# Output projection of a state-space layer: four full float32 products per tile become twelve reduced-precision ones

## What is computed

```
proj = rmsnorm(layernorm(x)) @ in_proj_w.T        # z 512, x_ssm 512, B 128, C 128, dt 8 columns
xc   = silu(conv4(x_ssm) + conv_b)                # per channel, four taps over time
dt   = softplus(dt_raw + dt_bias);  dA = exp(-exp(A_log) * dt)
h_t  = h_{t-1} * dA_t + (dt_t * xc_t) B_t ;  y_t = h_t C_t     # 8 heads of 64, state 128
y    = (y + D * xc) * silu(z)
out  = layernorm(x) + y @ out_proj_w.T            # 512 -> 256 channels; x = x + out
```

## Time and profile before

| | |
|---|---|
| runs | 1993.59, 1994.06, 1997.53 us; median 1994.06 |
| the profiled execution | 1994.79 us, its span (first to last instruction) 1992.6 us |
| PE, DVE, ACT, POOL busy in the span | 87%, 68%, 57%, 46% |
| state-space layer, first silu of xc to the end | 1411.5 to 1766.5 us |
| starts of the silu of xc (L1641) | 1411.49, 1458.08, 1504.23, 1550.39, 1596.53, 1642.69, 1688.91, 1733.92 us |
| granted clock of PE, mean | 0.961 of full speed |

### The profile page before, as it was taken

How to read it: one execution, slowest core, us unless ns; L and a number is a source line. 1 busy time by engine, 2 the same in 40 slices (tenths; PEclk the granted TensorE clock), 3 DMA queues, 4 the chain that set the end, 5 groups by cost and what they waited for, 6 DMA issues and landing times. The chain is left out here.

```text
span 1992.6 us, 30608 instructions
## 1 busy us (share of the span) xinstructions
PE 1740.4 (87%) x9553; PEld 1146.7 (58%) x9600; DVE 1364.6 (68%) x2907; ACT 1133.7 (57%) x1624; POOL 912.7 (46%) x621
## 2 busy tenths in 40 slices
PE   4999674899898998988899889997888888879998
PEld 3888564223222222225788767775666666657776
DVE  3544663677777777775545578885788887778886
ACT  3322463999999999995323222222777777622221
POOL 0001341899999999993000342211455444431111
PEclk9999887899999999999899989998999999989999
DMA  4000136424435352410000100000333222200000
GB/s 147 0 0 11 48 111 147 75 43 72 56 55 72 42 81 45 63 22 0 11 0 0 43 17 1 0 0 13 115 99 96 85 85 85 91 28 22 21 11 32
DMA packets 57638, 96.91 MB, mean 49 GB/s; under 512 B 7937, under 2 KB 29665, under 8 KB 57569
## 3 DMA queue, kind: packets, MB, share of 16 engines
q1 hardware_dynamic: 54752, 93.45, 20.8%
q10 hardware_dynamic: 2816, 2.60, 0.6%
HBM read 78.98 MB, written 17.04 MB: 48 GB/s over the span
## 5 line engine op out<-in xcount | busy, mean ns | idle before, releaser
L1217 POOL TENSOR_TENSOR att_weights<-att_weights 128x1024 f32<-128x1024 f32 x288 | 541.2, 1893 | 34.6 <-DVE att_weights L1161 23.6
L1161 DVE SCALAR_TENSOR_TENSOR att_weights<-att_weights,ps 128x512 f32<-128x512 f32 x576 | 370.2, 684 | 169.3 <-ACT att_weights L1136 167.5
L1132 ACT ACTIVATE att_weights<-ps 128x1024 f32<-128x1024 f32 x288 | 294.4, 1022 | 26.7 <-PE ps L1078 22.9
L1136 ACT ACTIVATE att_weights<-att_weights 128x1024 f32<-128x1024 f32 x288 | 302.5, 1051 | 0.0
L711 DVE SCALAR_TENSOR_TENSOR X<-ps,moe_gsel,X 128x256 f32 (+1 forms) x512 | 246.8, 484 | 66.5 <-PE ps L47 50.7
L1092 PE MATMUL ps<-att_weights,att_v_ones 128*32 128x512 f32 (+3 forms) x1536 | 288.7, 497 | 2.6 <-POOL att_weights L1217 2.5
L1075 PE MATMUL ps<-att_q_stack,att_k_stack 128*128 128x512 bf16 (+3 forms) x721 | 215.7, 334 | 51.6 <-DVE att_weights L1161 43.0
L1075 PEld LDWEIGHTS ps<-att_q_stack,att_k_stack 128*128 128x128 bf16 x768 | 74.3, 97 | 321.6 <-DVE att_weights L1161 285.0
L47 PE MATMUL ps<-w_experts_hi,moe_xh 128*128 128x512 f32 x512 | 206.2, 403 | 0.3 <-DVE X L711 0.3
L47 PE MATMUL ps<-w_experts_hi,moe_xl 128*128 128x512 f32 x512 | 203.9, 398 | 0.0
L47 PE MATMUL ps<-w_experts_lo,moe_xh 128*128 128x512 f32 x512 | 202.3, 395 | 0.0
(11 more groups left out here) (252 smaller groups left out, 3749.0 us busy)
## 6 DMA issues: line engine op xcount, KB each, us to landing
att_q_stack<-qk_parts SPq DMA_DIRECT2D x128, 128.0 KB, 4.6
ssm_lb<-decays SPq DMA_DIRECT2D x32, 512.0 KB, 4.8
ssm_rise<-decays SPq DMA_DIRECT2D x32, 512.0 KB, 3.9
att_k_stack<-qk_parts SPq DMA_DIRECT2D x120, 128.0 KB, 7.7
qk_parts<-qkv_part SPq DMA_DIRECT2D x32, 384.0 KB, 2.6
out<-X SPq DMA_DIRECT2D x8, 512.0 KB, 2.9
X<-in_x SPq DMA_DIRECT2D x3, 1024.0 KB, 5.7
load_raw<-in_ffn_w SPq DMA_DIRECT2D x8, 256.0 KB, 5.2
```

Of the source, the lines that this page charges most:

```text
L1132: act.activation(Wt[:, u % WU], scores(u), ACT.Exp).then_inc(exp_done, 1)
L1136: act.activation(Wt[:, u % WU], Wt[:, u % WU], ACT.Ln, bias=1.0).then_inc(ln_done, 1)
L1161: dve.scalar_tensor_tensor(out=wt[:, t], in0=wt[:, t], scalar=LIMIT, in1=scores(u)[:, t], op0=ALU.min, op1=ALU.max).then_inc(max_done, 1)
L1217: pool.tensor_tensor(Wt[:, u % WU], Wt[:, u % WU], Wt[:, u % WU], ALU.mult).then_inc(sq_pool, 1)
```

## The change

The weights of the output projection are kept as two F32R parts, `out_h` and `out_l`. They are loaded into the first slot of `dec`, and at the start of the layer ACT copies the high part and DVE subtracts for the low part. `y` becomes one slot. After `gate`, ACT copies `y` into `yh` (`high`), then DVE subtracts into `yl` (`remainder`) and signals `y_done`; `gate` itself signals `yg_done`. `tile_out` takes twelve products with 256 columns from the four parts. The wait for `out_done` moves from `gate` on DVE to `high` on ACT, and asks for the tile just before.

```diff
-        out_w, ones = sb("out_w", [P, FT, C]), sb("ones", [P, P])
+        ones = sb("ones", [P, P])
+        out_h, out_l = (sb(f"out_w_{part}", [P, FT, C], F32R) for part in ("hi", "lo"))
...
+        out_w = dec[:, 0].rearrange("p h t -> p (h t)").rearrange("p (f c) -> p f c", f=FT)
...
-        y = sb("y", [P, 2, FT, P])
+        y = sb("y", [P, FT, P])
+        yh, yl = (sb(f"y_{part}", [P, FT, P], F32R) for part in ("hi", "lo"))
...
-                for k in range(FT):
-                    ins = pe.matmul(ps_o, y[:, b % 2, k], out_w[:, k], start=k == 0, stop=k == FT - 1)
-                ins.then_inc(out_done, 1)
+                matmul3(pe, ps_o, lambda k: yh[:, k], lambda k: yl[:, k], lambda k: out_h[:, k],
+                        lambda k: out_l[:, k], range(FT)).then_inc(out_done, 1)
...
+            pe.wait_ge(out_split, 1)
             groups(pe, group)
...
+            def high(n, b):
+
+                act.wait_ge(yg_done, n + 1)
+                act.wait_ge(out_done, 2 + n)
+                act.activation(yh[:, :, :], y[:, :, :], ACT.Copy).then_inc(yh_done, 1)
+
...
                     if left and b == 0:
                         hi(p + 1)
+                    high(n, b)
                     if left and b:
                         piece(p + 1, 1 - v, b)
...
             act.activation(neg_a[:, :], neg_a[:, :], ACT.Exp).then_inc(init_done, 1)
+            act.activation(out_h[:, :, :], out_w[:, :, :], ACT.Copy).then_inc(oh_done, 1)
             hi(0)
...
+            act.wait_ge(out_split, 1)
             decays(0, 0, 0, 0)
...
                 dve.wait_ge(y_summed, n + 1)
-                dve.wait_ge(out_done, n + 1)
...
-                dve.tensor_tensor(y[:, b % 2], y[:, b % 2], zs[:, :, b], ALU.mult).then_inc(y_done, 1)
+                dve.tensor_tensor(y[:, :, :], y[:, :, :], zs[:, :, b], ALU.mult).then_inc(yg_done, 1)
+
+            def remainder(p, b):
+                n = p * GT + b
+                dve.wait_ge(yh_done, n + 1)
+                dve.tensor_tensor(yl[:, :, :], y[:, :, :], f32(yh[:, :, :]), ALU.subtract).then_inc(y_done, 1)
...
                     gate(p, v, b)
                     update_state(p, v, b)
+                    remainder(p, b)
...
+            dve.wait_ge(oh_done, 1)
+            dve.tensor_tensor(out_l[:, :, :], out_w[:, :, :], f32(out_h[:, :, :]), ALU.subtract).then_inc(out_split, 1)
             dve.wait_ge(init_done, 4)
             statistics(1)
```

More of the change, by code:

```diff
@@ L1403, in ssm_phase @@
                              "state_done", "h_decayed", "h_done", "out_done", "x_done"))
+        yg_done, yh_done, oh_done, out_split = (sem(n) for n in ("yg_done", "yh_done", "oh_done", "out_split"))
         FREE = 1
@@ L1755, in gate @@
                 dve.wait_ge(y_summed, n + 1)
-                dve.wait_ge(out_done, n + 1)
                 for f in range(FT):
-                    ins = dve.scalar_tensor_tensor(out=y[:, b % 2, f], in0=xc[:, v, f, b], scalar=d_col[:, f:f + 1],
+                    ins = dve.scalar_tensor_tensor(out=y[:, f], in0=xc[:, v, f, b], scalar=d_col[:, f:f + 1],
                                                    in1=ps_y[:, f * P:(f + 1) * P], op0=ALU.mult, op1=ALU.add)
```

## The result

| | runs of this comparison, us | median |
|---|---|---|
| before | 1993.59 to 2001.49 (4 runs) | 1995.8 |
| after | 2026.89 to 2030.37 (4 runs) | 2028.34 |

The changed kernel is slower: ratio 1.0159, 95% interval 1.0135 to 1.0184, 32.5 us between the medians. Its profiled execution took 2028.83 us with a span of 2027.0, 34.4 more than the earlier trace rows.

A forecast was written before the change was run, and what follows sets the result against it. It put PE on the path only in part, with gate hand-overs, ACT's order and DVE deciding elsewhere. 24.6 + 1.6 + 3.9 + 2.0 = 32.1 us on 1994.79 gave 2026.9, 2026 for the median; range 2019 to 2033.

The forecast's parts named there:

- six steady groups: Groups with a normalise: waits at tiles 0 to 3 and the end make each 4.1 us longer, 24.6 in all.
- the seventh group: Group without normalise: the copy of tile 3 waits only for its gate, +1.6 us.
- The last group: Nothing hides its hand-overs: four of 1.5 us, less 0.4, less about 1.7: +3.9, between 1.5 and 5.6.
- The product term: Output projection on PE: twelve split products at 0.12 us take 1.43 for 1.83, a gain of 0.40 us per tile.
- Tile 0: Steady group: tile_y(1) starts 1.5 us later behind copy and subtraction; decays(2), behind the copy on ACT, 3.7 later.
- Tile 1: Steady group: PE's units, tile_y(2), decays(3) and weigh(3) all at +1.1 us; DVE's idle 4.83 us hide the rest.
- Tile 2: Steady group: ACT reads the two x_ssm units only after gate and copy, +3.9 us; decays(4) and normalise slip too.
- The end of a group: Steady group: ACT is 4.7 us late at the silu of xc, but DVE at times_dt(0) sets the shift, +4.1.
- The fourth rival: The subtraction meets POOL on the path: 2.2 us more in each of six groups, 2039; 8%.
- less about 1.7: Last group: PE's waits of 1.60 us come from a 2.7 us multiply beside POOL, which the later gate partly escapes.
- The third rival: New waits around tile_out(3) lower PE's clock at each group's start: +10 us over six groups, 2036; 15%.
- The start of the layer: ACT's weight copy and DVE's subtraction stand ahead of statistics and first operands: +2.0 us, between 1.2 and 2.6.

The follow-up runs named there:

- e1: The kernel before with twelve F32R products, DVE's multiply writing y as F32R, no copy or subtraction, high part used for both: 1995.58 us, ratio 0.9995.
- e2: The changed kernel with copy, subtraction and their waits, but the four float32 products of before: 2029.62 us, ratio 1.0159.
- e5: The changed kernel with tile_y waiting for the gate's four additions, not for the end of the subtraction: 2018.35 us, ratio 1.0108.
- e7: As e5, with the projection of the tile before placed behind tile_state and turn_x on PE: 2017.07 us, ratio 1.0103.
- e9: As e2, with ACT's copy alone and no subtraction; the copy signals y_done: 2022.55 us, ratio 1.0137.
- e11: The changed kernel with POOL's long product cut to an eighth, the rest left out of the result: 2014.02 us, ratio to before 1.0085.
- e3: The changed kernel with ACT's copy of tile 2 moved behind the two units of x_ssm: 2026.02 us, ratio 1.0147.
- e10: As e2, with DVE's subtraction alone, reading y alone, and no copy on ACT: 2017.99 us, ratio 1.0109.
- e12: The kernel before with POOL's long product cut to an eighth, the rest left out of the result: 1984.96 us, ratio 0.9948.
- light pair: e11 and e12, the changed kernel and the one before with POOL's long product cut to an eighth: 2014.02 and 1984.96 us.
- e6: The kernel before with tile_y waiting for the gate's four additions, not for the multiply behind them: 1997.76 us, ratio 1.0008.

## Why the prediction was right

The time, 2026 for 2028.3, came out, and so did the mechanism of the six steady groups but for the engine that comes last in them. Part of the nearness is luck: in the profiled execution the six groups and the start were 3.5 us under their terms, the seventh group, the last and what stands ahead of the layer 5.9 over. The last group, 7.3 us, lies outside its own bounds of 1.5 to 5.6.

**The product term.** PE's gain per tile was 0.30 us and not 0.40: the 0.12 us between starts were right, but the first product costs 0.22. It changed little: by e1 the whole gain is worth 0.17 us a group.

**The chain, shown by its length.** In six kernels ACT has no gap from the copy of tile 2 to the silu, and this stretch is always 17.6 us. The group's length is then the end of the gate of tile 2 (all times after the group's silu) plus that stretch: after 32.16, e2 32.51, e5 31.12, e7 31.15, e9 31.83, e11 31.00, and the groups 49.79, 50.13, 48.75, 48.77, 49.45, 48.63. Each sum agrees within 0.03 us. Before, the gate ended at 31.57, nearly the same, but the stretch did not wait for it. That is the prediction's tile 2, "the wait that costs".

**Tile 0.** Measured from the group's silu, `decays(2)` started at 10.53 for 7.46. After starts each group 0.55 us sooner in one respect: `tile_y(0)` follows the silu at 4.82, not 5.37, since DVE no longer is last there. So +3.6, forecast +3.7. The wait of PE before `tile_y(1)` ended with the subtraction, as forecast.

**Tile 1.** exp of dt started at 22.03 for 21.46, +1.1 with the same 0.55 counted, as forecast; DVE's idle 4.83 us shrank to 1.64.

**Tile 2.** `normalise` at 39.03 for 35.92: +3.65, forecast +3.9.

**The end of a group: the wrong engine.** The prediction had ACT 4.7 late at the silu and DVE setting the shift at 4.1. ACT was 3.62 late and sets it; DVE, with `cb` at 49.19 for 46.11, was 3.08 late. With the 0.55 us counted, ACT was 4.2 and DVE 3.6 late, each half a microsecond under its forecast, and it is luck that DVE's forecast 4.1 is near ACT's 4.2. The 0.55 us that a group gets back at its start make 3.6 of that: 2.9 us less than forecast over six groups.

**The seventh group.** Forecast +1.6, since the copy of tile 3 has no `normalise` to wait for. It didn't, but the gate and a convolution met POOL:

```profile
1750.09 2.36 POOL L1863 TENSOR_TENSOR ssm_rise<-ssm_rise,ssm_cT 128x1024 f32<-128x1024 f32 x1
1750.20 2.79 DVE L1775 TENSOR_TENSOR ssm_y<-ssm_y,ssm_zs 128x512 f32<-128x512 f32 x1
...
1753.73 2.91 POOL L1863 TENSOR_TENSOR ssm_rise<-ssm_rise,ssm_cT 128x1024 f32<-128x1024 f32 x1 [1.28 <-DMA ssm_rise<-decays]
...
1754.63 4.14 DVE L1725 SCALAR_TENSOR_TENSOR ssm_xc<-ssm_xpad,ssm_conv_w,ssm_xc 128x512 f32<-128x512 f32 x3
```

These are 2.1 and 1.8 us over 0.69 and 2.32, with DVE last at the silu. They are not all new: before, the same multiply took 1.82, and the convolution and the small copy behind it at tile 2 took 2.98 and 2.32 for 2.32 and 0.17. Without these two the changed kernel has room for its hand-overs, and the gate's additions of tile 3 start 36.5 us after the silu in both kernels. From there the multiply is 1.0 longer, the subtraction with its wait adds 0.8, and the convolution is 1.8 longer: 3.6. The fourth rival looked for the collision at the subtraction, which after never shows (753 ns at the longest; in e3 and e10 it does). It fell on other instructions of DVE, in a group without its cover. In e11, without most of POOL's product, this group took 44.35 us for 48.58, in e12 42.38 for 45.01: by these runs the collisions are 1.6 of the 3.6, and 2.0 stay.

**The last group.** Forecast +3.9 (1.5 to 5.6), measured +7.3. The term was "four of 1.5", less 0.4, "less about 1.7". DVE after, at tiles 1 to 3:

```profile
1774.44 1.65 DVE L1756 TENSOR_TENSOR ssm_dec<-ssm_dec,ssm_cb 128x1024 f32<-128x1024 f32 x1 [2.07 <-ACT ssm_dec L1614]
...
1782.96 1.23 DVE L1756 TENSOR_TENSOR ssm_dec<-ssm_dec,ssm_cb 128x1024 f32<-128x1024 f32 x1 [1.74 <-ACT ssm_dec L1614]
1784.16 1.12 DVE L1770 SCALAR_TENSOR_TENSOR ssm_y<-ssm_xc,ssm_d_col,ps 128x128 f32<-128x128 f32 x4
...
1793.28 1.13 DVE L1770 SCALAR_TENSOR_TENSOR ssm_y<-ssm_xc,ssm_d_col,ps 128x128 f32<-128x128 f32 x4 [3.39 <-PE ps L1494]
```

- The hand-over of 1.5 is right at tile 0 and too short behind it. `decays(2)` and `decays(3)` stand behind the copies of tiles 0 and 1, and DVE's `weigh` and with it the gate wait for them, 2.07 and 1.74 us, where before the one wait of this kind was 0.60. The prediction had named this order for the steady groups and left it out here. In the light pair, where no `tile_y` up to these starts runs slow, `tile_y` to `tile_y` is 5.46, 7.75 and 7.75 us in e11 for 4.01, 5.12 and 4.79 in e12: +1.5, +2.6, +3.0.
- The "less about 1.7" came to 0.9: the multiply of tile 1 took 1.69 us for 2.69, that of tile 2 took 2.80 for 2.68.
- The clock was not in the term. PE after, at tiles 2 and 3, and `tile_y(3)` in e3, whose last group has the same order on every engine:

```profile
1780.44 0.70 PE L1491 MATMUL ps<-ssm_dec,ssm_xdt 128*64 128x128 f32 x4 [3.63 <-DVE ssm_y_lo L1780]
1780.89 0.67 PE L1494 MATMUL ps<-ssm_rise,ssm_H 128*64 128x128 f32 x4
...
1789.71 0.69 PE L1491 MATMUL ps<-ssm_dec,ssm_xdt 128*64 128x128 f32 x4 [2.19 <-DVE ssm_y_lo L1780]
```

```profile
1786.00 0.44 PE L1491 MATMUL ps<-ssm_dec,ssm_xdt 128*64 128x128 f32 x4 [2.30 <-DVE ssm_y_lo L1783]
```

The clock over that place and over a `tile_y` at full speed, from the windows view of the changed kernel (columns as above):

```profile
1781.00:1783.00 2.00, 2.00 (x22) 2.00 (x20) 0.26 (x2) 1.90 (x4) 0.00 (x0) 0.50 0.04 8
1773.00:1774.00 1.00, 1.00 (x18) 0.83 (x14) 0.00 (x0) 0.97 (x3) 0.04 (x1) 1.00 0.06 25
```

At tiles 2 and 3 the groups of four products start 0.42 us apart where 0.22 is usual, the granted clock is 0.50, 1.2 GHz, and a `tile_y` takes 3.26 us from its first start to its last for 1.70. `tile_y(0)` runs slow as well, but it did so before too; the mean clock of the window is 0.82, before 0.95. At tile 2 the slow clock costs nothing that the rows show: the additions at 1784.16 follow `weigh` without a gap. At tile 3 DVE waits for PE, and there e3 gives the price: its `tile_y(3)` ran at full clock, and from that start to the end of the layer it took 8.43 us where the changed kernel took 10.00. So of the 3.4 us missed the clock is 1.6, the multiply that did not escape POOL 0.8, and about 1 the `decays` behind the copies. e3 was not made to test this, and no experiment held the clock up.

The third rival had the mechanism and the wrong price. Behind PE's wait of 2.6 us `tile_y(3)` ran slow in four of the six groups too. Over the five from the second silu the mean clock was 0.97 in three and 1.00 in two, and they took 49.75 to 49.84 and 49.76 to 49.77 us: ACT's stretch ends later than PE there, and the +10 us did not come. In the seventh group, also at 0.50, DVE waited 0.84 us for this `tile_y`. Not each gap brought the low clock: in the last group of e9 `tile_y(2)` ran at full clock behind 3.86 us. The Trainium skill (TensorE: Matmul & The Clock Gate, Why this matters for your kernels) warns of idle gaps between bursts; the last group agrees with it, and e9 shows a gap that cost no clock.

**The start of the layer** was +1.4 to the first silu: copy 1.04 at 1381.14 and subtraction 1.23 at 1382.21 on ACT and DVE, statistics at 1383.35 for 1381.06, +2.3. Of these 0.5 stood ahead of the layer and 0.4 were covered.

## What to carry to other kernels

A saving on the busiest engine is worth nothing until some place shows that engine as the one that comes last: here 0.30 us of PE per tile bought 0.17 us a group, and a copy of 0.63 us with a subtraction of 0.69 cost 3.6 us a group. When a wait is put into an engine's written order, ask what stands behind it and where that stretch ends; an unbroken stretch like ACT's 17.6 us moves whole with its first instruction. Where two chains end within a microsecond of each other, relieving one shows only the small gap to the other, and parts tried alone (3.3 and 2.2 us) do not add up to the whole (4.0).

## What the runs showed of the hardware

- Twelve F32R products of 256 columns with weights that change at every product started 0.12 us apart, as in the earlier trace rows, but 0.22 behind the first; the four float32 ones took 0.46 each. Up to the next instruction the change of form is worth 0.30 of 1.83 us.
- DVE beside POOL: a 128x512 multiply of 0.69 us took 2.8, a convolution of three steps 6.85 for 2.32, a copy of 128x512 to F32R 2.28 for 0.42. The Trainium skill (SBUF — State Buffer, SBUF: two separate sides) has a VectorE instruction in a two-port mode or with two SBUF inputs and a GpSimd instruction exclude each other for a whole instruction. The multiply agrees: it started 0.1 us behind POOL's product of 2.36 us and ended 0.5 us after it. In which mode the copy ran no trace shows. An earlier start of PE's work, which lets POOL start earlier, made DVE's convolutions 2.0 and 4.5 us a group longer (e6, e5); in e6 the group grew by 0.6 us although a wait of PE had been removed.
- The copy to F32R took 0.42 us on DVE and 0.63 on ACT.
